# Two PSUM banks for the value product and two rotating ones, in the attention of a two-layer transformer kernel

## The reference, cut to what matters

```python
q = (x @ Wq.T).reshape(b, t, 16, 128).transpose(0, 2, 1, 3)
k = (x @ Wk.T).reshape(b, t, 4, 128).transpose(0, 2, 1, 3)
v = (x @ Wv.T).reshape(b, t, 4, 128).transpose(0, 2, 1, 3)
q, k = _qknorm(q, q_scale), _qknorm(k, k_scale)     # divided by the root mean square, scaled
k, v = jnp.repeat(k, 4, axis=1), jnp.repeat(v, 4, axis=1)
scores = jnp.einsum('bhtd,bhsd->bhts', q, k) * scale
attn = jax.nn.softmax(jnp.where(causal, scores, lowest), axis=-1)
out = jnp.einsum('bhts,bhsd->bhtd', attn, v)
return out.transpose(0, 2, 1, 3).reshape(b, t, 2048) @ Wo.T
```

## Time and profile before

| | |
| --- | --- |
| Median of 3 runs | 940.21 us (935.06 to 943.58) |
| The profiled execution | 945.97 us, its span 944.2 us |
| Attention with its projections | some 28 to 520 us of the span |
| TensorE busy | 805.1 us, 85% |
| VectorE busy | 587.1 us, 62% |
| ScalarE busy | 407.3 us, 43% |
| Mean granted clock of TensorE | 0.932 |

### The profile page before, as it was taken

One profiled execution on the slowest core, in us unless ns is written; L12 is line 12 of the kernel. 1 busy time (PEld: TensorE's weight loads), 2 busy tenths in 40 slices (PEclk: granted clock), 3 DMA queues, 4 the chain that ended last, 5 costly groups with the idle time before them and its releaser, 6 DMA issues.

```text
span 944.2 us, 13478 instructions
## 1 busy us (share of the span) xinstructions
PE 805.1 (85%) x4581; PEld 655.5 (69%) x4582; DVE 587.1 (62%) x1317; ACT 407.3 (43%) x912; POOL 227.5 (24%) x162
## 2 busy tenths in 40 slices
PE   4788999989999899998998787999996346999992
PEld 4576888877888778887887676777785143666661
DVE  5556768667686676866764765676768853333333
ACT  3356757657476574766663311222222011333330
POOL 1005201152001610013101503454530102333320
PEclk9988999999999999999999678999997756999997
DMA  4010000000001000000000814332304411111104
GB/s 178 1 34 0 2 1 1 35 23 1 1 1 35 24 1 1 2 1 23 1 1 1 320 27 143 99 101 93 103 36 182 175 45 33 41 44 41 45 17 133
DMA packets 16748, 48.32 MB, mean 51 GB/s; under 512 B 2445, under 2 KB 7950, under 8 KB 15536
## 3 DMA queue, kind: packets, MB, share of 16 engines
q1 hardware_dynamic: 13440, 41.37, 12.4%
q0 software_dynamic: 2208, 5.12, 1.9%
q10 hardware_dynamic: 1040, 1.05, 0.4%
HBM read 43.07 MB, written 5.37 MB: 51 GB/s over the span
## 4 chain that ended last, share of the span: by engine, by line
PE 66%; DVE 22%; issue 4%; ACT 4%; DMA 3%; POOL 0%; DVEq 0%; SPq 0%; POOLq 0%; ACTq 0%
PE ps L1199 14%; PE ps L1200 13%; PE ps L1201 12%; PE ps L1523 9%; PE ps L1541 4%; PE ps L1297 4%; DVE hid_lo L949 3%; DVE mx L850 3%; DVE pT_lo L864 2%; DVE o_f L918 2%; PE ps L1375 1%; PE ps L1209 1%; DVE stat L765 1%; PE ps L1363 1%; PE ps L1533 1%
## 5 line engine op out<-in xcount | busy, mean ns | idle before, releaser
L588 ACT ACTIVATE prob<-ps,negb,rqs 128x128 f32<-128x128 f32 (+7 forms) x128 | 106.7, 833 | 55.9 <-DVE negb L855 53.5
L577 ACT ACTIVATE pT_hi<-ps 128x512 fp32r<-128x512 f32 (+1 forms) x192 | 88.6, 488 | 72.7 <-PE ps L1297 66.8
L850 DVE TENSOR_REDUCE mx<-ps 128x1 f32<-128x128 f32 (+7 forms) x128 | 96.5, 754 | 31.3 <-PE ps L1289 30.3
L448 POOL TENSOR_TENSOR oT_lo<-o_f,oT_hi 128x512 fp32r<-128x512 f32 x32 | 41.3, 1289 | 293.1 <-ACT oT_hi L650 293.1
L864 DVE TENSOR_TENSOR pT_lo<-ps,pT_hi 128x512 fp32r<-128x512 f32 (+1 forms) x192 | 100.2, 550 | 7.0 <-ACT pT_hi L577 6.4
L1199 PE MATMUL ps<-pT_hi,v_hi 128*128 128x512 f32 x192 | 73.2, 381 | 21.9 <-DVE o_f L918 21.4
L1523 PE MATMUL ps<-wgu,xgT 128*128 x184 | 89.3, 610 | 1.0 <-ACT xgT L712 1.0
L1297 PE MATMUL ps<-ident,prob 128*128 128x128 f32 x576 | 86.5, 277 | 0.7 <-DVE qT_lo L884 0.4
L1199 PE MATMUL ps<-kT_hi,qT_hi 128*128 128x512 f32 (+1 forms) x192 | 70.6, 368 | 5.0 <-ACT prob L588 3.3
L666 ACT ACTIVATE th<-ps 128x512 f32<-128x512 f32 x34 | 20.3, 597 | 115.5 <-PE ps L1201 115.4
L1200 PE MATMUL ps<-kT_lo,qT_hi 128*128 128x512 f32 (+1 forms) x192 | 67.4, 351 | 0.0
(11 more groups left out here) (255 smaller groups left out, 2026.9 us busy)
## 6 DMA issues: line engine op xcount, KB each, us to landing
wbc<-combine SPq DMA_DIRECT2D x16, 512.0 KB
wgu<-in_gate_up SPq DMA_DIRECT2D x8, 1024.0 KB, 12.5
w_raw<-in_ffn SPq DMA_DIRECT2D x17, 384.0 KB, 8.4
wdn<-in_down SPq DMA_DIRECT2D x1, 4096.0 KB, 16.9
wqkv_raw<-in_w_attn SPq DMA_DIRECT2D x4, 768.0 KB, 4.2
wo_raw<-in_w_out SPq DMA_DIRECT2D x4, 512.0 KB, 3.3
x<-in_x ACTq DMA_DIRECT2D x1, 1024.0 KB, 7.1
wmod<-in_wmod SPq DMA_DIRECT2D x1, 1024.0 KB, 9.9
```

The lines of the kernel that those rows point to most:

```text
L448: nc.gpsimd.tensor_tensor(oT_lo[:, m % HPG, :], o_f[:], oT_hi[:, m % HPG, :], ALU.subtract).then_inc(oT_lo_done, 1)
L577: nc.scalar.activation(pT_hi[:, unit % NUNITS, 0:nb, qi * P:(qi + 1) * P], ps[:, ROTATING[place % 3], 0:nb * P].rearrange("p (j t) -> p j ...
L588: nc.scalar.activation(prob[:, n % 3, 0:w], ps[:, pair:pair + 2, :].rearrange("p b k -> p (b k)")[:, 0:w], ACT.Exp, bias=negb[:, n % 2:n % ...
L850: nc.vector.reduce_max(mx[:, i:i + 1], ps[:, pair:pair + 2, :].rearrange("p b k -> p (b k)")[:, 0:w], AX.X).then_inc(row_max, 1)
```

## The change

The value product gets banks 6 and 7, used in turn by even and odd heads, and the rotation keeps banks 4 and 5. Place p now waits for place p - 2, and the first piece of head m for o_f of head m - 2. The order of the work, `BANK_ORDER`, and all instructions other than their bank and these waits are the same.

```diff
-ROTATING = (4, 5, 7)
+ROTATING = (4, 5)
 PV_BANK = 6
...
-                    nc.vector.tensor_tensor(o_f[:], ps[:, PV_BANK, :], r_sb[:, m % 2, :], ALU.mult).then_inc(o_normed, 1)
+                    nc.vector.tensor_tensor(o_f[:], ps[:, PV_BANK + m % 2, :], r_sb[:, m % 2, :], ALU.mult).then_inc(o_normed, 1)
...
             def bank_free(place):
 
-                if place < 3:
+                if place < 2:
                     return
-                kind, index = BANK_ORDER[place - 3]
+                kind, index = BANK_ORDER[place - 2]
...
                 pe.wait_ge(pT_lo_done, FIRST_UNIT[m] if r == 0 else WHOLE_HEAD[m])
-                if r == 0 and m >= 1:
-                    pe.wait_ge(o_normed, m)
+                if r == 0 and m >= 2:
+                    pe.wait_ge(o_normed, m - 1)
...
-                    ins = three(ps[:, PV_BANK, q0:512], v_hi[:, t, :], v_lo[:, t, :], pT_hi[:, u, j % 4, q0:512],
+                    ins = three(ps[:, PV_BANK + m % 2, q0:512], v_hi[:, t, :], v_lo[:, t, :], pT_hi[:, u, j % 4, q0:512],
```

More of the change, by code:

```diff
@@ L577, in probs_high @@
                 nc.scalar.activation(pT_hi[:, unit % NUNITS, 0:nb, qi * P:(qi + 1) * P],
-                                     ps[:, ROTATING[place % 3], 0:nb * P].rearrange("p (j t) -> p j t", j=nb),
+                                     ps[:, ROTATING[place % 2], 0:nb * P].rearrange("p (j t) -> p j t", j=nb),
                                      ACT.Copy).then_inc(pT_hi_done, 1)
@@ L633, in _ @@
                 for kind, index, detail, place in BANK_AT[n]:
-                    bank = ROTATING[place % 3]
+                    bank = ROTATING[place % 2]
                     if kind == "kv":
@@ L1296, in transpose_probs @@
                 for j in range(nb):
-                    ins = nc.tensor.transpose(ps[:, ROTATING[place % 3], j * P:(j + 1) * P],
+                    ins = nc.tensor.transpose(ps[:, ROTATING[place % 2], j * P:(j + 1) * P],
                                               prob[:, k % 3, (j0 + j) * P:(j0 + j + 1) * P], ident[:])
```

## The result

The changed kernel takes 986.7 us (median of 4 runs, 985.02 to 993.08) against 939.23 us (4 runs, 935.06 to 943.58: the three of the table above and one more): ratio 1.0498, 95% interval 1.0441 to 1.0555, 47 us slower.

What follows compares the result with a forecast made beforehand. TensorE was taken to bound the attention. Net bank stalls of 55 us, between 48.7 and 60.1, plus 3 us for the clock gave 58 us on 940.2: 998 us, range 968 to 1024 (8 in 10).

Steps and rivals of the forecast that it cites:

- The lower bound: Attention: bank releases move with their step's scores and VectorE first catches up; 67.5 us lost, 19.0 given back, net 48.7.
- What the value bank gives back: First pieces of heads, waiting for o_f: 13.3 us in 31 heads, up to 19 if VectorE catches up.
- What the rotation costs: Places waiting for a bank's read-out with two rotating banks: 17.4 us of stalls in one group of heads.
- the steps with three groups: Steps 83, 87, 91, 95: third group waits for the first group's bank; 6.4 us, including key transposes in 95.
- The places behind a group of their own step: Steps 80, 84, 85, 88, 89, 92: query transpose, key projection or row-sum transpose waits for that group's bank; 4.8 us.
- the short steps 64 to 76: Steps 64, 65, 67, 68, 70, 71, 76, with projections among the groups, stall for banks: 6.2 us.
- The upper bound: Attention: late groups' hi and low parts delay the place after next again; 79.1 us less 19.0, net 60.1.
- The clock: Attention: more stalls lower TensorE's share from 93% to some 83%, adding 3 us at half speed.
- Faster (5%): Rival: bank waits in the attention vanish and only the o_f gain stays; 927 us, chance 5%.
- mostly absorbed (13%): Rival: only three-group-step stalls stay, VectorE absorbs the rest; 947 us, 13% together with cases up to 975.
- the clock (14%): Rival: granted clock falls to 0.89 over 520 us of attention, adding 38 us; 1033 us, chance 14%.
- The signs: Profile after: o_f waits under 2 us, pT_lo waits 65 to 80, head-group windows about 131, TensorE's busy time unchanged.

## Why the prediction came near, and where it was off

- **TensorE sets the pace and nothing behind absorbs a delay: right.** The attention grew by 47.2 us, the median by 47.
- **The lower bound was met by luck.** I worked it out as 67.5 us for the rotation less 19.0 for the value bank (48.5, where I wrote 48.7). In the attention the rotation alone cost 58.5 and the value bank gave 11.2. One term is 9 us too dear (6 with the 3.3 us of clock from above), the other 8 us too generous, and the difference hides both.
- **What the value bank gives back: the mechanism right, the size read right and then overrated.** The comparison place by place gave 13.3 us; one value bank against two measured 13 in the medians and 11.2 in the attention. I had let it grow to 19.0 with a catch-up of VectorE. That catch-up was small: in step 90 VectorE begins its maximum 1.81 us behind the scores (405.93 against 404.12) where it was 2.82 before, but in step 74 the low part comes no earlier against TensorE than it did, and the first pieces still wait 7.1 us in all. Of the 21.9 us that stood ahead of first pieces 14.8 went, some of it through the rotation's own shifts: the 0.20 us of step 90 are gone with one value bank too.
- **What the rotation costs: the right places, the sum a little too dear.** For all groups of heads I gave 67.5 to 79 us; the kernel with the rotation alone lost 58.5 in the attention and 61 in all. In the third group every listed step but 80 stalls, and besides them 69 (0.27 us) and 72 (0.55). With 0.16 us for each stall (below) the steps with three groups come to 5.7 us (idle 1.42, 1.21, 1.28 and 1.01) where I had 6.4; in step 95 no stall for the bank of the key transposes came. The places behind a group of their own step come to 4.3 us for 4.8 (query transposes of 85 and 89: 1.01 and 1.09), the short steps 64 to 76 to 8.3 us for 6.2. These are 18.3 us, of which 2.3 stood there before as other waits: 16.0 for my 17.4. The first pieces gave 3.7 us for the 4.5 or so that my 131 us for the window imply. The net of 12.3 us agrees with the 12.2 by which the window grew, but at equal clock it grew by some 13.4 and the second group's by 13.6, so the list of stalls is about 1 us short. I had forecast some 131 us for the window; it takes 130.3.
- **The upper bound: not needed.** That late groups delay the next but one place again was to add 11.6 us. The loss as measured, 47.2 us, lies under even the bound without it, 48.7; at equal clock it is some 2 us over that. My 55, the net of both terms, was a middle between two ends, and it is the term of the sum that was mis-sized, by 8 us as measured and by some 4.5 at equal clock.
- **The clock: wrong sign.** I added 3 us. The granted clock in the first window rose from 0.95 to 0.97, and over the attention TensorE spent 13.7 us at the lower level against 17.1. TensorE's share of the window from 290 to 320 us fell to 89% (98% in the earlier trace rows) and the clock stayed at 1.00. Behind 55 us it was at the lower level once, for 3.4 us, as often as in the kernel before behind 85 us. By the rule that I cited from the Trainium skill (TensorE: Matmul & The Clock Gate, "A second HAM failure mode: psum-queue depth-cycling") it would swing between its levels; with stalls of up to 1.3 us here it did not.
- **The rivals.** Faster (5%), mostly absorbed (13%) and the clock (14%) are all refuted: 77.3 us of idle time in the attention, at a granted clock of 0.97 to 1.00.
- **The signs.** The o_f waits are gone and the windows take 130.3 us, as said. The waits for low parts of probabilities are 50.0 us and not 65 to 80; the idle times in steps with three groups are 1.0 to 1.4 us and not 1.2 to 1.6. VectorE's maximum starts within 0.2 us of the scores in 64 of 128 steps (51 before) and over 1 us behind them in 24 (29 before), which is not nearly everywhere. The stages behind the attention, 420.5 us, lie among the 419.0 to 426.2 us of all kernels here. One sign was made badly. TensorE's busy time in the attention, the second number of these rows (before, then changed), grew by 10.4 us, over the 10 that were to mean a fallen clock, while the clock rose (0.98 to 0.99):

```profile
28.80:518.60 489.80, 450.71 (x2912) 387.80 (x2912) 336.14 (x782) 304.43 (x712) 94.59 (x58) 0.98 0.03 9
25.70:562.80 537.10, 461.12 (x2912) 387.08 (x2912) 338.99 (x782) 308.88 (x712) 94.74 (x58) 0.99 0.03 8
```

The last section shows where these 10.4 us come from.

## What to carry to other kernels

Before a buffer is taken from a rotation, compare for each place when its writer starts now with when the place that would have to be free is read out, and count only what the places before have not already shifted: here that named the right steps and put the cost of the rotation at 67.5 us where the attention lost 58.5. Cost and gain need a run each, since two errors can cancel in the difference. A buffer is held not by its reader's own 0.3 us but by what stands ahead of the reader on its engine, here a 1.2 us maximum; if the bank must go, try to move that, and look at what it delays in turn (here it gave back about a fifth of the loss, and with three banks the same order cost 7 us). A resource that is idle in some steps (here half of each score pair) can give a part of the second buffer's gain without the price: 7 us here, where a bank of its own gave 13 and cost 61.

## What had not been expected of the hardware

A stall costs TensorE more than its idle time shows. Matmuls of 512 columns are listed with 0.39 us but start 0.23 us apart (step 91 of the changed kernel):

```profile
411.10 0.39 PE L1200 MATMUL ps<-pT_lo,v_hi 128*128 128x512 f32 x1
411.33 0.40 PE L1201 MATMUL ps<-pT_hi,v_lo 128*128 128x512 f32 x1
```

So the last one before a stall is listed as busy for 0.16 us longer than its turn. Idle time in the attention grew by 37.3 us (40.0 to 77.3, with 46 and 111 gaps over 0.1 us), the attention by 47.2; the rest, 9.9 us, is 0.15 us for each of the 65 gaps more, and somewhat more at equal clock. Single steps say the same: step 91 takes 1.49 us longer than before for an idle time of 1.28, step 92 0.64 for 0.45. The windows show it as busy time: 113.60 us in the third group where the same instructions had 111.41, and 65 times 0.16 us are the 10.4 us by which the attention's busy time grew. Starts of instructions give the price of a stall, idle sums fall short of it by a fifth.
